# Attention in a two-layer network: key and query loads regrouped, first maxima moved into the projections, row DMAs issued by ScalarE

## The reference

```
x = x + 0.5 * L0_ffn(layernorm(x));  x = x + L0_attn(layernorm(x));  x = x + 0.5 * L0_ffn(layernorm(x))
x = x + 0.5 * L1_ffn(layernorm(x));  x = x + L1_attn(layernorm(x));  x = x + 0.5 * L1_ffn(layernorm(x))

L0_attn: q, k, v = split(x @ W_qkv), 16 heads of 16;  softmax(q k^T / 4 + alibi + causal mask) v, then @ W_o
L1_attn: the same with biases and rotary position (x * cos + x_shift * sin) on q and k, no alibi
```

## Time and profile before

| what | us |
|---|---|
| median of 3 runs (lowest, highest) | 1870.79 (1869.03, 1882.45) |
| profiled execution | 1878.28 |
| its span | 1876.0 |
| PE busy | 1573.3 (84%) |
| DVE busy | 1281.3 (68%) |
| ACT busy | 950.2 (51%) |
| POOL busy | 306.5 (16%) |
| DMA | 70.55 MB, 38 GB/s over the span |

### The profile page before, as it was taken

How to read it: one execution, slowest core, us unless ns; L and a number is a source line. 1 busy time by engine, 2 the same in 40 slices (tenths; PEclk the granted TensorE clock), 3 DMA queues, 4 the chain that set the end, 5 groups by cost and what they waited for, 6 DMA issues and landing times. The chain is left out here.

```text
span 1876.0 us, 33089 instructions
## 1 busy us (share of the span) xinstructions
PE 1573.3 (84%) x13356; PEld 985.2 (53%) x13356; DVE 1281.3 (68%) x1859; ACT 950.2 (51%) x1889; POOL 306.5 (16%) x327
## 2 busy tenths in 40 slices
PE   1588637999999999787799587599999999997996
PEld 0477524444434445676588565344444344356886
DVE  8665525888898851664599764468878988414997
ACT  3344303667778886444334221146577787862432
POOL 5333000000000000232044322000000000011334
PEclk9999867999999999898899788579889999998998
DMA  5000893100000000100000058710000000010000
GB/s 193 23 1 1 165 187 58 32 23 14 23 13 12 2 2 1 46 0 23 34 1 1 14 102 167 122 30 20 19 21 11 12 11 2 2 68 1 12 12 23
DMA packets 37635, 70.55 MB, mean 38 GB/s; under 512 B 5189, under 2 KB 12997, under 8 KB 36422
## 3 DMA queue, kind: packets, MB, share of 16 engines
q1 hardware_dynamic: 37494, 68.58, 16.0%
HBM read 48.90 MB, written 22.15 MB: 38 GB/s over the span
## 5 line engine op out<-in xcount | busy, mean ns | idle before, releaser
L1096 DVE TENSOR_REDUCE l_att_maxima<-psum 128x2 f32<-128x1024 f32 (+3 forms) x640 | 665.2, 1064 | 179.9 <-PE psum L1006 170.7
L1181 ACT ACTIVATE l_att_probs<-psum 128x512 f32<-128x512 f32 (+3 forms) x1280 | 605.0, 531 | 255.6 <-PE psum L1026 232.8
L1043 PE MATMUL psum<-l_att_probs,l_att_v 128*17 128x256 f32 (+2 forms) x4608 | 358.5, 384 | 1.2 <-ACT l_att_o L1188 0.7
L1026 PE MATMUL psum<-l_att_qt,l_kt 51*128 51x512 f32 (+6 forms) x1280 | 330.1, 465 | 7.5 <-ACT l_att_probs L1181 7.5
L1006 PE MATMUL psum<-l_kt,l_att_qt 59*128 59x512 f32 (+7 forms) x1280 | 289.4, 430 | 5.3 <-DVE l_att_maxima L1096 3.8
L1026 PEld LDWEIGHTS psum<-l_att_qt,l_kt 59*128 59x128 f32 (+1 forms) x1280 | 143.8, 192 | 168.8 <-ACT l_att_probs L1181 151.9
L1043 PEld LDWEIGHTS psum<-l_att_probs,l_att_v 128*17 128x17 f32 x4608 | 78.9, 96 | 148.5 <-issue 98.1
L1006 PEld LDWEIGHTS psum<-l_kt,l_att_qt 59*128 59x128 f32 (+1 forms) x1280 | 141.7, 204 | 19.8 <-DVE l_att_maxima L1096 18.8
L1149 POOL CAST l_att_crow<-l_att_cneg 128x16 bf16<-128x16 f32 x32 | 8.1, 252 | 868.8 <-DVE l_att_cneg L1107 868.8
L1003 PE MATMUL psum<-tri 64*128 64x128 bf16 x1024 | 90.2, 241 | 44.8 <-DMA l_att_qt<-qx_alibi 17.2
L1024 PE MATMUL psum<-tri 64*128 64x128 bf16 x1024 | 82.9, 229 | 21.0 <-DMA l_att_qt<-l_att_ct 20.8
(11 more groups left out here) (199 smaller groups left out, 2933.4 us busy)
## 6 DMA issues: line engine op xcount, KB each, us to landing
qk_scratch<-l_att_kv_parts SPq DMA_DIRECT2D x32, 512.0 KB, 13.8
l_kt<-qk_scratch SPq DMA_DIRECT2D x48, 256.0 KB, 9.5
l_att_qt<-qk_scratch SPq DMA_DIRECT2D x156, 64.0 KB
l_att_qt<-qk_scratch SPq DMA_DIRECT2D x12, 192.0 KB
set_raw<-in_w_gu SPq DMA_DIRECT2D x2, 1024.0 KB, 6.3
x_resident<-in_x SPq DMA_DIRECT2D x1, 2048.0 KB, 15.3
y<-in_w_gu SPq DMA_DIRECT2D x1, 2048.0 KB, 7.4
raw_down<-in_w_dn SPq DMA_DIRECT2D x2, 1024.0 KB, 8.4
```

Source lines behind the costliest of these rows:

```text
L1026: e.matmul(g.ps[:, i % SB, off:BLK], g.kt[rows_of(x), hp, kt * P:(kt + 1) * P], qt[rows_of(x), hp, off:BLK], start=u >= TPB, stop=True, sk ...
L1043: ins = e.matmul(g.ps[h * VW:h * VW + HD + 1, OB, lo:hi], g.v[:, kt, STEPS[st][1] * HG + h, :], pr[:, un % PB, h, lo:hi], start=u == 0 and ...
L1096: e.tensor_reduce(mp[:, st % 2, 2 * p:2 * p + 2, t, c], g.ps[:, bank:bank + 2, 0:w], AX.X, ALU.max).then_inc(s.mx, 1)
L1181: e.activation(pr[:, un % PB, h, off:BLK], g.ps[:, i % SB, off:BLK], ACT.Exp, scale=HD ** -0.5).then_inc(s.ex, 1)
```

## The change

What it does, in the order of the diff:

- `xh`, `xl` get two buffers; transposes of the next block stand behind m = 2, its high part on ACT behind the third high part, its low part on DVE behind the last rotation (layer 1) or the third remainder (layer 0). Layer 0 has 6 slots of parts instead of 5. Layer 1's tables have two buffers, loaded a block ahead.
- Among the stores SP issues only `load_k(0)`, the first queries and the rest of query block 0; `load_k(1)` to `load_k(3)` follow all stores.
- The 8 products and maxima of step 0 stand inside the last block's projections (AHEAD), in banks 0 and 1, one at a time. `maxima_rows(0)` stands behind two products of step 1 instead of behind all 16.
- ACT issues the two row DMAs of each step itself, behind a wait for its own copy.
- At each place the maxima products, rows and output stand ahead of the scores.

```diff
-    NS = 6 if rope else 5
+    NS = 6      # own slots, in layer 0 four of them in the spare space of g.y
+    g.xh, g.xl = sb("xh", [P, 2, KD, BLK], F32R), sb("xl", [P, 2, KD, BLK], F32R)
...
+                if is_last(b):
+                    first_products(m)
+                elif m == 2:
+                    transposes(b + 1)
...
+                if is_last(b):
+                    first_products(NM + j)
-            if not rope and not is_last(b):
-                transposes(b + 1)
...
+                if m == 2 and not is_last(b):
+                    act_hi(e, g, s, b + 1, half=(b + 1) % 2)
...
         for b in range(NB):
+            if rope and b < NB - 1:
+                if b:
+                    e.wait_ge(s.za, 2 * NM * b)
+                tables(b + 1)
             for m in range(NM):
...
-                if m == 0 and b:
-                    load_k(b - 1)
-                if m == 1 and b == NB - 2:
+                if b == 1 and m == 0:
+                    load_k(e, 0)
+                if b == 1 and m == 1:
                     first_queries(e, 0)
-                if m == 1 and b == NB - 1:
+                if b == 2 and m == 0:
                     first_queries(e, 1)
-        load_k(NB - 1)
...
+        AHEAD = (0, 0, 1, 1, 1, 1, 2, 2)
+        EARLY = mbase[1] + 2
...
+                elif k:
+                    e.wait_ge(s.mx, k)
...
+            def first_products(i):
+                for k in ahead(i):
+                    max_products(k, 0)
...
+                    elif i < 2:
+                        e.wait_ge(s.mx, mbase[1])
...
-            for k in range(due(0)):
+            kv.tensor(e, first_products)
+            for k in range(mbase[1], EARLY):
                 max_products(k)
             maxima_rows(0)
+            for k in range(EARLY, due(0)):
+                max_products(k)
             for p in range(PLACES):
-                if p < 2 * UNITS:
-                    scores(p // 2, p % 2)
                 for k in range(due(p), due(p + 1)):
                     max_products(k)
...
+                if p < 2 * UNITS:
+                    scores(p // 2, p % 2)
                 if p >= LAG:
                     values((p - LAG) // 2, (p - LAG) % 2)
...
                 e.activation(ctt[:, :], psb[0:MROWS * HG, 0:BLK], ACT.Copy).then_inc(s.ctc, 1)
+                e.wait_ge(s.ctc, st + 1)
+                hg = STEPS[st][1]
+                for r in range(2):
+                    e.dma_start(qt[r * HALF + mrow:r * HALF + mrow + MROWS, hg * HG // 2:(hg + 1) * HG // 2, :].bitcast(F32),
+                                ctt[r * MROWS * HG // 2:(r + 1) * MROWS * HG // 2, :].bitcast(F32)).then_inc(s.cdma, 16)
...
-                    if h == 0 and un == 1:
-                        kv.parts_stored(e)
...
             kv.sync(e, first_queries)
-            rows(0)
+            for b in range(1, NB):
+                kv.load_k(e, b)
             for st in range(NS):
                 qb, hg = STEPS[st]
-                if st < NS - 1:
-                    rows(st + 1)
```

More of the change, by code:

```diff
@@ L772, in body @@
                     rotate(b, m)
+                    if m == NM - 1 and not is_last(b):
+                        dve_lo(e, g, s, b + 1, half=(b + 1) % 2)
                     if m:
@@ L776, in body @@
                     remainder(b, m)
[L777 removed]
+                    if m == 2 and not is_last(b):
+                        dve_lo(e, g, s, b + 1, half=(b + 1) % 2)
+                if not is_last(b) and m == 0:
                     dve_normalise(e, g, s, b + 1)
+                if is_last(b):
+                    first_maxima(m)
             if rope:
                 remainder(b, NM - 1)
[L781 to L782 removed]
+            if b + 2 < NB:
+                dve_stats(e, g, s, b + 2)
+            if is_last(b):
+                for j in range(TPB):
+                    first_maxima(NM + j)
         dve_layernorm(e, g, s, 0)
@@ L807, in gpsimd, with load_k @@
             body(b)
+    def load_k(e, b):
+        for c in range(NM // 2, NM):
+            e.wait_ge(cp[slot(b, c)], stored(b, c))
+        for sec in range(SECS):
+            src = a["qk_scratch"][K_PARTS[sec], 1, :, ds(b * BLK, BLK)].rearrange("(h r d) t -> r d h t", r=2, d=HD)
+            for r in range(2):
+                row = r * HALF + section(sec)
+                e.dma_start(g.kt[row:row + HD, :, ds(b * BLK, BLK)].bitcast(F32), src[r]).then_inc(kl[b], 16)
     def sync(e, first_queries):
@@ L890, in attention_phase @@
         g.v = sb("v", [P, NT, HEADS, HD + 1], F32)
-        with ExitStack() as before:
-            kv = projections(nc, g, f"{name}_kv", rope, a, lambda n, shape, dt: sb(f"kv_{n}", shape, dt, before), splits, small)
-        mrow = XROW + g.bias_rows
-        PB = 3
         mp = sb("maxima", [P, 2, HG, TPB, NB], F32)
@@ L899, in attention_phase @@
         ctt = sb("ct", [MROWS * HG, BLK], F32R)
+        with ExitStack() as before:
+            kv = projections(nc, g, f"{name}_kv", rope, a, lambda n, shape, dt: sb(f"kv_{n}", shape, dt, before), splits, small)
+        mrow = XROW + g.bias_rows
+        PB = 3
         osb = sb("o", [P, BLK], F32)
@@ L964, in slot_bank, with ahead @@
             return SB + 2 * (r % 2)
+        def ahead(i):
+            return range(sum(AHEAD[:i]), sum(AHEAD[:i + 1]))
         block = ctx.enter_context(nc.Block())
@@ L1123, in normalise @@
                 read += 1
-            for k in range(due(0)):
+            kv.vector(e, first_maxima)
+            for k in range(mbase[1], EARLY):
                 maxima(k)
             ring += 1
+            for k in range(EARLY, due(0)):
+                maxima(k)
             for p in range(PLACES):
```

136 lines of the change are left out of this document (70 added, 66 removed).

## The result

| | before | changed |
|---|---|---|
| median (lowest, highest), 4 runs each | 1875.12 (1869.03, 1882.45) | 1955.14 (1951.23, 1966.93) us |
| span of the profiled execution | 1876.0 | 1952.9 us |
| mean granted clock of TensorE | 0.917 | 0.886 |

The ratio is 1.0436, 95% interval 1.0373 to 1.0498. I had forecast 1852 and a range of 1822 to 1886: the changed kernel is slower by 80 us, and the prediction was wrong.

The account below looks back on a forecast made before the run. It took DMA to bound the way to layer 0's first scores and the steps to be balanced without slack. Profiled 1878.3 - 53 + 34 = 1859, or 1852 on the median (1870.8 - 19), range 1822 to 1886.

Parts of the forecast that it names:

- part 1: Way in: three key loads moved behind the stores take 39 us of queue out of the first scores' way.
- The anchor: First maxima of step 4, first work needing key block 1: from 323.19 to 303 (layer 0), 1236.91 to 1202 (layer 1).
- the two limits: Layer 0's step 4 maxima: 300.8 by compute and 300.4 by the queue, taken together as 303, 20 us gained.
- My queue limit: SP's in-order DMA queue: step 4's maxima can't come before all earlier traffic plus a query load, 300.4 and 1198.5.
- Part 2: Projections: each block shrinks by about 4.5 us; lost again in layer 0, layer 1's way in 35 us shorter.
- Part 3: Steps: ACT's two row issues cost net 1.25 us a full step, 27.5 plus 6.4 for early steps, 34 us lost.
- Part 4: Steps: maxima products ahead of scores keep a place at 1.22 us; taken as 0, 3 us either way.
- The cyclic argument: At each place, scores, products, values becomes scores, values, products: same 1.22 us and same distances, so no cost.
- the way in: Stretch up to step 4's first maxima in each layer: 53 us gained in all, bounds 35 and 61.
- A: Rival, steps: the row issue costs ACT little, up to 12 us; 1818 to 1830, say 1824; chance 0.22.
- B: Rival, first scores: rows don't pass the key loads, gains 2 and 16 instead of 53; 1892, slower; chance 0.12.
- C: Rival, way in: queries behind bunched key loads come later still, gain only 35; 1870, no change; chance 0.14.

Follow-up runs that it names:

- run 5: Changed kernel with scores first, all row DMAs on SP, step 0's ahead of key load 1, key loads 2 and 3 spread behind later queries: 1812.67 us, ratio 0.9696.
- run 1: Kernel before, with one edit: ACT issues both row DMAs of each step behind its copy: 1961.09 us, ratio 1.0491.
- run 4: Changed kernel with scores first again and the rows of steps 4 to 15 sent by SP, those of steps 0 to 3 by ACT: 1839.06 us, ratio 0.9813.
- run 3: Changed kernel with the scores put back ahead of products, rows and output; ACT still issues the rows: 1900.32 us, ratio 1.0139.
- 11: Changed kernel with products first kept and only the rows of steps 4 to 15 given back to SP: 1881.29 us, ratio 1.0043.
- run 12: Changed kernel, PE repeating the scores' first product four times in the place behind each row copy (22 places, steps 5 to 15): 1924.25 us, ratio 1.0234.

## Why the prediction was wrong

**What bounds it; part 1, loads regrouped: the number right in layer 0, by luck.** The anchor came at 303.55 (said 303), 19.6 us gained (said 20). But of the two limits only one acted: there is no idle time of PE for a query load at the anchor. I had written that without it the queue wouldn't be served in order; that doesn't follow. In the changed kernel SP issued the bunched key loads and then the queries of (1, 0) 25 us later:

```profile
246.64 16.15 SPq L845 DMA_DIRECT2D l_kt<-qk_scratch  x18
287.68 2.63 SPq L1285 DMA_DIRECT2D l_att_qt<-qk_scratch  x6
```

By then the queue had run empty (DMA share 1.04 in the window 275 to 280 us, 0.34 in the next, 0.13 in the one behind), since step 0's scores, for which the queries wait, were themselves late by the rows. My queue limit had no such gap in it, and the number came out by compute. That was luck: two errors cancel in it. DVE was done with step 0's maxima at 257.8 us and not at 265, and the scores came 16 us behind that and not 7 (the second line is layer 1's, for part 2):

```profile
257.81 0.18 DVE L1164 TENSOR_REDUCE l_att_cneg<-l_att_maxima 128x16 f32<-128x16 f32 x1
...
1195.86 0.18 DVE L1164 TENSOR_REDUCE l_att_cneg<-l_att_maxima 128x16 f32<-128x16 f32 x1
```

Also, the window from which I took 257 GB/s for stores alone has SP's first key load in it, from 212.86, so it isn't a rate of stores alone.

**Part 2, compute ahead: the blocks right, layer 1 wrong.** DVE's `xl` remainders in layer 1 of the changed kernel:

```profile
1109.00 1.29 DVE L158 TENSOR_TENSOR l_att_kv_xl<-psum,l_att_kv_xh 128x512 fp32r<-128x512 f32 x2
...
1125.89 1.28 DVE L158 TENSOR_TENSOR l_att_kv_xl<-psum,l_att_kv_xh 128x512 fp32r<-128x512 f32 x2
...
1143.99 1.28 DVE L158 TENSOR_TENSOR l_att_kv_xl<-psum,l_att_kv_xh 128x512 fp32r<-128x512 f32 x2
```

16.9 and 18.1 us apart, 17 predicted, 21.5 before. Yet the first scores of layer 1 came 28 us earlier instead of 41, and the anchor 17.5 instead of 35. Of the 13 us that the scores lack, 11 are the way of the rows: I had put 7 us for POOL, transposes, copy, issues and flight, and from the end of the maxima (1195.86) to the scores (1214.22) it was 18.4. In layer 0 of run 5, with the rows ahead of the key loads, the issue and the flight took 4.6. Behind the scores the anchor took 36.4 us and not 26.2, and there the clock was lower. The 44 us behind the first scores of layer 1, changed and then before:

```profile
1214.00:1258.00 44.00, 40.65 (x342) 22.46 (x342) 19.31 (x25) 15.82 (x39) 1.99 (x8) 0.50 0.33 50
```

```profile
1210.71:1254.71 44.00, 40.90 (x444) 23.07 (x446) 27.60 (x36) 20.15 (x51) 2.00 (x8) 0.73 0.09 23
```

PE is as busy in both, but gets 342 matmuls done and not 444. I had written of cold stretches that they "cost some 2 us", from no row; steps 1 to 4 of layer 1 took 94 us against 67.

**Part 3, rows issued by ACT: mechanism and price right, size wrong by two.** The source view of the changed kernel answers to the earlier trace rows:

```profile
L1239 ACTq DMA_DIRECT2D l_att_qt<-l_att_ct x64: 725/726/1362, 260.6 to 1678.4; - x64
```

0.726 us an issue, 1.3 us a full step at full clock, as worked out. Predicted were 34 us; runs 1, 4 to 3 and 11 to the changed kernel measured 84, 61 and 74. Of run 1's 71 us in the span 39 are 30 copies at 1.3. Another 5 stand in layer 0 before ACT's first issue, where PE's wait for the queries ends at 285.04 and not at 280.15, so they aren't the edit's:

```profile
285.04 0.40 PE L1003 MATMUL psum<-tri 64*128 64x128 bf16 x4 [20.54 <-DMA l_att_qt<-qx_alibi]
```

About 27 are left, 25 of them in steps 1 to 15 (which hold 26 of the copies), where 17 of 30 steps are below clock 1.00 (8 before). That this rest is the clock is read from the windows. I had put 6.4 us on the copies of steps 1 to 4 of both layers; the steps 1 to 4 as cut, which hold the copies of steps 3 to 5, grew by 16 in run 1 (11.1 and 5.3), clock included. What the clock does behind such a stall I had priced at nothing. The Trainium skill (DMA: Bandwidth & Descriptors, Issuing engines are not separate DMA queues) calls the issue time usually small beside the DMA itself; in these runs ACT's issues cost 3 to 5% of the kernel, as they stand in the list of an engine that has no slack in the full places.

**Part 4, products first: the step that failed.** "The same 1.22 us" holds for a place in the middle of a step at full clock, and from it I took 0 for the order. It measured 0.8 us in a step of 32 places (0.6 in one of 24), by my estimate from the steps at full clock some 15 to 18 us over 30 steps, and 41 to 55 us on the median. The cyclic argument looked at one kind of place; at the two ends of a step (the places behind the output, and the masked ones ahead of the next step) the cycle isn't the same. Why it is dearer there stays open.

**Forecast and rivals.** The forecast was -53 for the way in, +34 for the issue and 0 for the order, in sum -19. Undone one after the other (changed kernel, run 3, run 4, before) the parts measured +55 for the order, +61 for the issue, and -38 for all the rest. Of the 99 us between forecast and result the order has 55, the issue 27 and the way in 15; 2 are left, by which the kernel before differed on the two chips. A (the issue is cheap) is false. Of B, slower, the place was right: the first scores did wait for the rows while the key loads ran, 7.8 and 10.1 us, though in layer 0 the loads weren't done by then. But its price was far too small, and it isn't what made the kernel slow, as run 4 has the same wait and is faster than before. C's way in of 35 us is near the 37 measured at the anchors, but not by its mechanism: PE waited for no queries there. The wrong terms, parts 3 and 4, are both delays of about a microsecond put some 30 times into PE's list; for the first I summed the waits and left out the clock, for the second I put nothing. Filling the gaps gives 31 us back, which can't be time saved at full clock, since the steps at 1.00 didn't get shorter (step 10 of layer 0: 35.43 and 35.62); so about this much was lost by the clock. That the remaining growth of steps 1 to 7 (57 us, at clocks of 0.50 to 0.87 in most) is the clock too is argued from the windows, and wasn't tried.

## What to carry to other kernels

When a stage keeps three engines within 15% of each other, a microsecond inserted once per step must be priced twice: by its own length, and by what TensorE's granted clock does afterwards; here the second came out about as large as the first. Compare step lengths at equal clock before blaming an instruction, and compare the clock column before blaming anything else. Take a bundle apart: here two parts cost 3 to 5% and 2 to 3%, the loads among them gained 2%, and the good half alone, with the rows kept on SP and the key loads spread, beats the kernel before by 3% and the changed one by 7%.

## What the runs showed of the hardware

**More work can be faster.** With 22 filled places the changed kernel went from a ratio of 1.0436 to 1.0234 (run 12). What a single fall of the clock costs is seen in run 1. In step 11 of layer 1, the first 11.5 us look like those of the kernel before, then the clock is 0.51 for 20.8 us, and full again:

```profile
1531.45:1537.45 6.00, 5.00 (x66) 2.48 (x64) 5.69 (x7) 2.68 (x7) 0.00 (x0) 1.00 0.00 0
1537.45:1542.90 5.45, 5.26 (x58) 2.39 (x56) 4.91 (x6) 3.24 (x9) 0.00 (x0) 1.00 0.01 2
1543.00:1563.80 20.80, 20.45 (x124) 7.53 (x128) 13.29 (x14) 9.85 (x20) 1.01 (x4) 0.51 0.01 1
1563.90:1573.39 9.49, 9.49 (x114) 3.73 (x106) 7.58 (x8) 8.23 (x17) 0.00 (x0) 1.00 0.16 47
```

In the first 6 us PE is idle for 1.0. The kernel before has the same 5.01 of 6.00 at the same place (1471.86 to 1477.86), and 5.25 of 5.44 behind it, and keeps its clock, so the idle time just ahead doesn't decide alone. ACT's last issue (1518.97) lies 24 us ahead of the fall. The Trainium skill (TensorE: Matmul & The Clock Gate, A second HAM failure mode: psum-queue depth-cycling) says that short idle times between groups of matmuls can make the clock change between its levels; this trace shows such a change and its price, 6.5 us for one such stretch (41.94 against 35.44), but not that the idle times are what sets it off. That isn't settled.

**A small DMA on another queue didn't overtake much.** The 12 KB rows of step 0, issued by ACT from 260.57 to 262.69 while SP's 18 key loads were in flight, let the scores start 11.2 us after the last issue. On SP's own queue with no load just ahead of them (run 5) the exponentials, later than the scores, began 4.1 us after the last issue. From the first issue to the scores it was 13.3 us on ACT's queue beside 18 key loads, 9.5 on SP's queue right behind one key load (288.21 to 297.75, kernel before), and 4.6 on SP's queue ahead of the loads (run 5). What ran on the DMA engines when the rows were issued counted for more than the queue; whether the second queue helped at all isn't shown.
